# A third of a mixture-of-experts stage moved beside the node pass in front of it

## The reference

```python
xn = layernorm(x)
x  = x + gnn(xn, edges) + mix(xn)          # graph attention; linear attention
z  = layernorm(x) * gamma + beta           # gamma, beta of the expert layer
logits = z @ Wr + br                       # 8 experts
top_vals, top_idx = top_k(logits, 2)
w = softmax(top_vals)
for e in range(8):
    h = gelu(z @ W1[e] + b1[e])            # 256 -> 512
    y = y + (h @ W2[e] + b2[e]) * w_of(e)  # 512 -> 256
out = x + y
```

## Time and profile before

| | us |
|---|---|
| median of 3 runs (lowest to highest) | 3553.38 (3551.12 to 3561.58) |
| the profiled execution | 3556.23, of which the span from first to last instruction 3554.6 |
| busy over the span | PE 2799.0, DVE 2343.5, POOL 2154.7, ACT 1273.4 |
| the pass, with the list and the start of the expert part | 2266 to 2770 |
| the expert part | 2770 to the end |

### The profile page before, as it was taken

The page is one execution under the profiler, slowest core; times in us unless marked ns, Lnnn a source line. Parts: engine busy times, 40 slices in busy tenths (PEclk is TensorE's granted clock), DMA queues, the critical chain, the costliest instruction groups (busy, mean ns, idle before and its releaser), DMA issues. The chain is left out here.

```text
span 3554.6 us, 70140 instructions
## 1 busy us (share of the span) xinstructions
PE 2799.0 (79%) x17326; PEld 2288.6 (64%) x17327; DVE 2343.5 (66%) x6416; ACT 1273.4 (36%) x4243; POOL 2154.7 (61%) x2117
## 2 busy tenths in 40 slices
PE   6758888889989978888888888433344899999997
PEld 4635666666666756666666666323334799999997
DVE  6656666666666667777777777888877455555554
ACT  5723333333333323333333333355542233333332
POOL 3167777777777776666666666246666344444443
PEclk9979999999999989999999999755555899999999
DMA  7645656666666666666666666445582344444443
GB/s 248 240 130 156 159 158 160 161 159 162 163 163 164 162 157 185 180 177 182 178 175 174 171 174 171 130 158 177 183 281 103 74 70 71 71 71 69 72 71 52
DMA packets 384652, 529.69 MB, mean 149 GB/s; under 512 B 64276, under 2 KB 323559, under 8 KB 384218
## 3 DMA queue, kind: packets, MB, share of 16 engines
q0 software_dynamic: 114496, 265.49, 31.9%
q1 hardware_dynamic: 185112, 183.84, 17.5%
q10 hardware_dynamic: 84770, 77.19, 6.8%
HBM read 394.80 MB, written 132.72 MB: 148 GB/s over the span
## 5 line engine op out<-in xcount | busy, mean ns | idle before, releaser
L1133 POOL DMA_INDIRECT rows<-node_rows,index x1552 | 1476.2, 951 | 566.3 <-issue 447.5
L1411 PE MATMUL ps_sum<-msg,hot 128*128 128x260 f32 x3904 | 1015.0, 405 | 18.4 <-DVE big L1230 2.6
L1411 PEld LDWEIGHTS ps_sum<-msg,hot 128*128 128x128 f32 x3904 | 727.5, 196 | 133.1 <-issue 7.8
L1213 DVE TENSOR_TENSOR msg<-rows,ps_w 128x1024 f32<-128x1024 f32 x488 | 595.9, 1221 | 38.0 <-ACT ps_w L1305 22.4
L2123 POOL DMA_INDIRECT out_dram<-big x204 | 353.1, 1731 | 437.2 <-DVE big L2215 388.0
L2174 ACT ACTIVATE x_actT<-x_ps_hT,b1T 128x128 f32<-128x128 f32 x816 | 232.8, 368 | 523.8 <-PE x_ps_hT L2149 523.8
L1189 DVE TENSOR_SCALAR hotT<-targets,pair_node_id 128x512 bf16 x488 | 187.0, 383 | 344.3 <-SPq L1095 340.5
L2149 PEld LDWEIGHTS x_ps_hT<-x_rowsT,x_w_now 128*128 128x128 f32 x3264 | 399.0, 193 | 11.5 <-DVE x_w_now L2193 1.1
L1391 PE MATMUL ps_hot<-ident_h,hotT 128*128 128x128 bf16 x1952 | 194.9, 223 | 268.2 <-DVE hotT L1189 266.0
L2149 PE MATMUL x_ps_hT<-x_rowsT,x_w_now 128*128 128x128 f32 x3264 | 400.1, 276 | 0.7 <-DVE x_w_now L2193 0.7
L1700 POOL DMA_INDIRECT expert_in<-f_rows,f_slot x196 | 259.4, 1323 | 223.7 <-ACT f_rows L1742 166.7
(11 more groups left out here) (284 smaller groups left out, 4146.7 us busy)
## 6 DMA issues: line engine op xcount, KB each, us to landing
targets<-dst_row SPq DMA_DIRECT2D x391, 128.0 KB
big<-expert_in SPq DMA_DIRECT2D x204, 130.0 KB, 2.1
rows<-node_rows,index POOLq DMA_INDIRECT x1564
node_rows<-big SPq DMA_DIRECT2D x14, 924.0 KB
turned<-rT SPq DMA_DIRECT2D x14, 896.0 KB, 4.5
area<-turned ACTq DMA_DIRECT2D x98, 128.0 KB
queries<-area ACTq DMA_DIRECT2D x98, 128.0 KB
area<-queries ACTq DMA_DIRECT2D x98, 128.0 KB
```

The lines of the kernel that those rows point to most:

```text
L1133: g.indirect_dma_start(rows[:, j, k, :], None, s.node_rows, bass.IndirectOffsetOnAxis(ap=index[:, b, j * G + k:j * G + k + 1], axis=0)).th ...
L1213: v.tensor_tensor(m[:, :, 0:D].rearrange("p g (h f) -> p g h f", h=GH), rows[:, bass.ds(here, 1), :, 0:D].rearrange("p j g (h f) -> p (j g ...
L1411: mm = pe.matmul(ps_sum[:, j % 2, 0:SUM], hot[:, j % MSGS, k * P:(k + 1) * P], msg[:, j % MSGS, k, :], start=(k == 0), stop=(k == G - 1))
```

## The change

`finish` and `run_experts` become one function, `pass_and_experts`, with one program for each engine. When seven of the fourteen chunks have been placed, DVE lists 17 blocks of 512 rows of one expert each (`list_quads`, at the end of step 8). These 17 blocks are 68 expert tiles. They run beside steps 9 to 16. Each step has ten positions, and a table says how many tiles (0, 1 or 2) go at each; all five engines use it, so that the tile's instructions stand between those of the pass:

That makes 3, 44, 8, 6 and 7 tiles in steps 9, 10 to 13, 14, 15 and 16. The orders of ACT and PE become:

```diff
+                for n in range(CHUNKS + 3):            # ACT
+                    for p in range(1, 11):
+                        if 2 <= n < CHUNKS + 2 and p <= CHUNK + 1:
+                            make_row(n - 2, p - 1)
+                        if n < CHUNKS:
+                            if p == 4:
+                                gat_root(n)
+                            if p >= 5:
+                                scale_tile(n, p - 5)
+                            if p == 10:
+                                scale_tile(n, CHUNK - 1)
+                        if p == 10 and 1 <= n <= CHUNKS:
+                            ffn_root(n - 1)
+                        if p == 10 and 2 <= n < CHUNKS + 2:
+                            odds_of(n - 2)
+                        first_tiles([look_up, gelu], [0, 1], n, p)
+                later_tiles(act, [look_up, gelu], [0, 1])
...
+                steps, lag = [look_up_later, turn_rows, down, up], [0, 0, 3, 1]
+                for n in range(1, CHUNKS + 3):         # PE
+                    for p in range(1, 11):
+                        if 2 <= n < CHUNKS + 2:
+                            if p <= CHUNK + 1:
+                                turn_row(n - 2, p - 1)
+                            if p == 10:
+                                rank(n - 2)
+                        first_tiles(steps, lag, n, p)
+                    if n <= 4:
+                        for e in range(2 * n - 2, 2 * n):
+                            fold_bias(e)
```

`turn_row(c, i)` waits for the row that `make_row(c, i)` writes in the same position, and for the copy of the row before it; the buffer `ps_t` that they share is now single:

```diff
+                def turn_row(c, i):
+                    t = c * CHUNK + i
+                    if i < CHUNK:
+                        pe.wait_ge(rows_ready, t + 1)
+                    if t >= 1:
+                        pe.wait_ge(rowsT_ready, t)
```

DVE puts a tile's work behind each of its eight larger pieces of a step (after the product, the sum, the statistics and the moments of `divide`, and likewise in `join`) and twice behind `choose`. Weights of a block come through a ring of two, and DVE scales W1 in place, once for each block:

```diff
+                def load_quad_w1(q):
+                    e = quad_expert_now(q)
+                    if q >= 2:
+                        sp.wait_ge(hT_psum, QUAD * (q - 1))
...
```

```diff
+                        if p == 7 and n <= CHUNKS + 1:
+                            if n >= 2:
+                                settle_homes(n - 1)
+                            if n <= CHUNKS:
+                                store(n - 1)
+                            if n < CHUNKS:
+                                load_hx(n)
+                            if n + 1 < CHUNKS:
+                                load_xn(n + 1)
```

More of the change, by code:

```diff
@@ L1476, in _, with pass_and_experts @@
                           (MIX_AT, 4, project_out), (MIX_AT, 2, turn_heads), (MIX_AT, 0, attend)])
-def finish(nc, s, x, ln_gamma, ln_beta, w_norm2, gamma, beta, Wr, br, W1, b1, W2, out):
+def positions():
+    at = {}
+    it = 0
+    for n in range(CHUNKS + 3):
[10 more added lines that the diff above has]
+                count = 1 if p < 10 else FIRST
+            else:
+                count = 0
+            count = min(count, FIRST - it)
+            at[n, p] = range(it, it + count)
+            it += count
+    assert it == FIRST
+    return at
+TILES_AT = positions()
+def pass_and_experts(nc, s, x, ln_gamma, ln_beta, w_norm2, gamma, beta, Wr, br, W1, b1, W2, b2, out):
     with ExitStack() as ctx:
@@ new lines, in up @@
+                def up(n, j, turn):
+                    if early(n):
+                        u = n // QUAD % 2
+                        pe.wait_ge(quad_scaled, 2 * (n // QUAD + 1))
+                    else:
+                        u = j % 2
+                        pe.wait_ge(w1_ready, n - (FIRST - 1))
+                    pe.wait_ge(x_rowsT_ready, n + 1)
+                    from_item(pe, act_ready, n, 2, n - 1)
+                    for k in range(HC):
+                        for c in range(C):
+                            a = c * HID + k * P
+                            mm = pe.matmul(ps_hT[:, j % 2, k * P:(k + 1) * P], w_ring[:, u, a:a + P], x_rowsT[:, j % 2, c, :],
+                                           start=(c == 0), stop=(c == C - 1))
+                    mm.then_inc(hT_psum, 1)
@@ new lines, in down @@
+                def down(n, j, turn):
+                    if early(n):
+                        q = n // QUAD
+                        if n % QUAD == 0:
+                            pe.wait_ge(quad_w2_in[q % 2], 16 * (q // 2 + 1))
+                    else:
+                        if isinstance(n, int) and n == FIRST:
+                            pe.wait_ge(experts_in, EXPERT_LOADS)
+                        e = expert(n, j)
+                    pe.wait_ge(act_ready, n + 1)
+                    from_item(pe, out_ready, n, 2, n - 1)
+                    for c in range(HC):
+                        if early(n):
+                            w = w_ring[:, q % 2, C * HID + c * D:C * HID + (c + 1) * D]
+                        else:
+                            w = w2[:, bass.ds(e, 1), c * D:(c + 1) * D].rearrange("p e n -> p (e n)")
+                        mm = pe.matmul(ps_out[:, j % 2, 0:D], actT[:, j % 2, c, :], w, start=(c == 0), stop=(c == HC - 1))
+                    mm.then_inc(out_psum, 1)
@@ L1800, in _ @@
[L1800 removed]
+                pe.wait_ge(consts, 6)
+                pe.wait_ge(router_set, 2 * C + 1)
+                steps, lag = [look_up_later, turn_rows, down, up], [0, 0, 3, 1]
+                for n in range(1, CHUNKS + 3):
+                    for p in range(1, 11):
+                        if 2 <= n < CHUNKS + 2:
[7 more added lines that the diff above has]
+                            fold_bias(e)
@@ L1802, in _ @@
+                later_tiles(pe, steps, lag)
             @block.vector
             def _(v):
+                look_up, expert = expert_registers(v, "dve")
                 done = [0]
@@ L1811, in settle, with now @@
                     v.wait_ge(chain, done[0])
+                def now(ins):
+                    then(ins)
+                    settle()
                 def over_experts(a):
```

794 lines of the change are left out of this document (454 added, 340 removed).

## The result

The changed kernel took 3541.04 us (median of 5 runs, 3533.42 to 3548.77), the kernel before 3561.58 beside it (5 runs, 3551.12 to 3565.12, the three known before the prediction among them). The ratio is 0.995, with a 95% interval of 0.9931 to 0.9968: faster by 0.5%, little, but clear of the runs' scatter. The prediction had 3576 and slower as the likeliest sign.

A forecast was written before the change was run, and what follows sets the result against it. DVE was taken to set the pass steps and PE the expert part. 2552.7 + 38 + 316 + 56 + 46 + 29 + 10 + 530 = 3577.7 us, 23 over the old span, giving 3576; range 3490 to 3650.

The forecast's parts named there:

- Before step 9: Everything ahead of step 9: 11.6 us of list on DVE, 8.4 and 4 of other delays, 24 us more in all.
- The homes: Steps 5 to 7: `settle_homes` puts 1 MB ahead of the transfer `divide` waits for, 2.8 us each, 8.4 in all.
- the folds: Ends of steps 2 to 4: they hold PE while ACT's rows and the root wait, 0 to 8 us, taken as 4.
- A mixed step by position: Steps 10 to 13, ten positions of pass and tile work: most 6.78 us, sum 68.7, with lost clock 79.1.
- The lock: Mixed steps: `up`, gelu, row, copy and PE's next turn follow one another, leaving PE idle 2.47 us in a 6.78 us position.
- Rival 3: Mixed steps: PE and ACT don't bind each other, a step lasts as its busiest engine, 50 us; total 3430; chance 0.08.
- The clock: Mixed steps: each of eight idle PE gaps loses 1.3 us to a lower clock, 10.4 a step; chance 0.50.
- The table load: Position 10 of a mixed step: three ACT table loads of 1.28 us counted, in a position of 9.5 us.
- list of signs: Trace signs for steps 10 to 13: PE gaps near 2.5 us, five table loads, steps of 75 to 85 us, clock 0.6 to 0.9.
- Rival 1: Mixed steps: the clock holds in the short gaps, 57 us less, span 3521, median 3520, 0.9% faster; chance 0.24.
- The other steps: Outside steps 10 to 13: step 9 38 us, steps 14 to 16 56, 46 and 29, behind the list 10, from tile 68 530.

## Why the prediction was wrong, point by point

**Before step 9.** 24 us were predicted, 10.3 came. The list begins on DVE at 2519.95 and step 9 at 2532.36: 12.4 us against 11.6. The homes (8.4) and the folds (4) cost nothing: `divide` waited 19.0 us for `xn` in the first nine steps, where the kernel before waited 21.5 for its load. I had added the homes to the transfer that comes last; that `divide` now waits for `xn` alone, and not for `hh` and `x_row` too, I had not taken off. Which of the two kept the balance was not tried.

**A mixed step by position.** The lock is there as predicted, 6.73 us a position against 6.78, and both runs that break it take 16 us from a step in the mean. Rival 3 falls for the changed kernel; its price was near: broken, the lock gives 3440 to 3450, where the rival had 3430.

**The clock: the step that failed.** The prediction said "Together 2.47 us of idle PE" and took 1.3 us of lost clock for every such gap, 10.4 a step with the long one. The gap was 2.19 us, and none of the 20 short gaps of steps 10 to 13 lost the clock; only the two long ones of a step did, and it took 71.7 us and not 79.1. The length was put together badly from the earlier trace rows. `up` starts at 2802.75 and takes 1.95, so it ends 0.17 us after PE's next turn has begun at 2804.53; I measured the gelu's start from the turn, 0.30, where `up`'s end gives 0.13. And the gelu counted with its duration, 1.14, where the next row starts 1.02 behind its start; for the row I had used start to start (0.49 of 0.59). What the gap lost the work gained, so the position came out right and hid the error. The price itself was of the right size: with gaps of 2.49 us the three steps cost (82.1 - 73.8) + 3.4 for the two stretches that the changed kernel has, 11.7 us by eight gaps, 1.5 a gap, and the kernel stood at 3577. The length is not all of it, though. Gaps of 2.49 us held the clock in one step of three, and those of 2.18 and 2.19 lost it in step 13 of the run without gelu's table. So it is shown that the changed kernel's short gaps cost nothing in the profiled execution, and that 0.3 us more on each brings the price; why all of them held stays open.

**The table load.** The prediction's list of signs names five table loads in a step, and there are five, but its sum has only the three at position 10. `gat_root` at position 4 needs another table, and gelu's own comes back behind the wait for `up`, in the lock: 1.26 us in each mixed step, and the gap of 3.45 that loses the clock. Rival 1 is what happened, but its price lacked this, and the low stretches behind the two long gaps: a step of 68.7 us against 71.7, a span of 3521 against 3531.7. Both long gaps and their stretches together are 7 us a step (71.7 against 64.5 without gelu's table).

**The other steps.** Step 9 took 36.1 us (38), steps 10 to 13 2855.2 - 2568.5 = 286.7 (316; step 14 is counted from 1.4 us ahead of PE's first row, as that lies in the steps before), the rest to tile 68 142.4 (56 + 46 + 29 + 10 = 141), tile 68 to the end 534.1 (530). Of the 46 us between the predicted and the measured span, 29 are steps 10 to 13, 13.6 the part before step 9, 6.7 the edge stage; the rest gives 3 back.

**The rule on gaps.** The earlier trace rows and the windows of the changed kernel show which gaps lost the clock: 2.95, 3.45 and 5.14 us, while those of 2.19 did not. The Trainium skill's rule ("TensorE: Matmul & The Clock Gate", section "Why this matters for your kernels"), by which short idle gaps don't cost the clock, held for the changed kernel. It did not hold for many of the gaps of 2.49 and 2.67 us in the runs above, nor for those of 2.18 and 2.19 in step 13 of the run without gelu's table, all shorter than the page puts the bound: there the runs decide.

## What to carry to other kernels

When work is mixed position by position, look for a place where one engine's next input stands behind its own last output on another engine; the step is then as long as that chain, however idle the engines are, and moving either end by one position frees it (16 us of 72 here, until the transfers are late). Where a price hangs on a gap's length, take the length from start to start, with the end of a pipelined matmul by its own duration, and forecast both sides if the row that shows a loss is within half a microsecond; gaps of one length can keep the clock in one step and lose it in the next. Before crediting an overlap, run its tiles one after the other with everything else kept: here that was faster (3516) than the overlap with the lock (3541), and slower than the overlap without it (3440 to 3450).

## What the runs showed of the hardware

- The longer the repeated gaps, the more of them lost the granted clock, but no length here divides them. In steps 10 to 13 none of 20 gaps of 2.18 to 2.31 us lost it in the changed kernel; with gaps of 2.48 and 2.49 us 8 of 19 did, with 2.67 to 2.81 us 10 of 20, with 3.65 us all 20. Without gelu's table four of six gaps of 2.18 and 2.19 us lost it in step 13, and one of 3.37 kept it in step 10. At 2.49 us a lost gap costs 3.1 us in a position of 7.03.
- In this kernel a table load comes behind the wait of the activation that needs it: at position 4 ACT was idle for 3.28 us, then loaded gelu's table for 1.28. The activation followed 0.02 us behind the load.
- In the run with the late gelu PE waited 13.2 us for the load of one expert tile, which SP issued behind its transfers of position 7; the DMA engines' busy share was 0.81 in that step.
